# A token-routed FFN behind a graph convolution: second half of the first weights held back, and eleven unread matmuls

## What is computed

```python
logits = jnp.einsum('bsd,ed->bse', tgt, Wr) + br
top_v, top_i = jax.lax.top_k(logits, 2)          # 8 experts, 2 for each token
top_w = jax.nn.softmax(top_v, axis=-1)
...
h = jax.nn.relu(jnp.einsum('bsd,efd->bsef', tgt, W1) + b1)   # 1024 -> 512
o = jnp.einsum('bsef,edf->bsed', h, W2) + b2                 # 512 -> 1024
tgt2 = jnp.einsum('bsed,bse->bsd', o, router_w)
return _layer_norm(tgt + tgt2, gamma, beta)
```

## Time and profile before

| | us |
|---|---|
| median of 3 runs | 2134.6 |
| lowest, highest | 2126.74, 2134.81 |
| the profiled execution, its own time | 2129.83 |
| its span | 2128.1 |
| mean granted clock of TensorE | 0.974 |

### The profile page before, as it was taken

The page is one execution under the profiler, slowest core; times in us unless marked ns, Lnnn a source line. Parts: engine busy times, 40 slices in busy tenths (PEclk is TensorE's granted clock), DMA queues, the critical chain, the costliest instruction groups (busy, mean ns, idle before and its releaser), DMA issues. The chain is left out here.

```text
span 2128.1 us, 27953 instructions
## 1 busy us (share of the span) xinstructions
PE 2011.7 (95%) x9385; PEld 1600.0 (75%) x9385; DVE 1252.4 (59%) x2316; ACT 986.1 (46%) x1541; POOL 924.6 (43%) x813
## 2 busy tenths in 40 slices
PE   7999999999999999999989999899889949999994
PEld 6777777777777777887868767677568748888883
DVE  7589868952222222216989988888978852222237
ACT  3211122222222222227999999999934313333346
POOL 0000036555565655406777877878700012221226
PEclk9999999999999999999999999999989959999997
DMA  5322277777777777768788989989947679999747
GB/s 188 105 81 79 71 241 254 253 264 257 248 262 249 251 252 252 255 204 292 262 315 286 324 283 330 338 303 319 329 152 225 201 294 330 312 295 310 239 133 166
DMA packets 156360, 521.55 MB, mean 245 GB/s; under 512 B 31362, under 2 KB 31746, under 8 KB 154186
## 3 DMA queue, kind: packets, MB, share of 16 engines
q1 hardware_dynamic: 83706, 308.63, 41.6%
q0 software_dynamic: 72528, 211.35, 32.4%
HBM read 385.49 MB, written 156.25 MB: 255 GB/s over the span
## 5 line engine op out<-in xcount | busy, mean ns | idle before, releaser
L221 PE MATMUL psum<-w_hi,xnT_hi 128*128 128x512 f32 (+1 forms) x1592 | 420.2, 398 | 9.9 <-issue 5.0
L221 PE MATMUL psum<-w_lo,xnT_hi 128*128 128x512 f32 (+1 forms) x1592 | 419.5, 394 | 0.0
L221 PE MATMUL psum<-w_hi,xnT_lo 128*128 128x512 f32 (+1 forms) x1592 | 413.0, 394 | 0.0
L590 ACT ACTIVATE work<-psum 128x512 f32<-128x512 f32 (+1 forms) x150 | 89.9, 599 | 673.0 <-PE psum L221 673.0
L924 POOL DMA_INDIRECT sorted_rows<-acc x313 | 340.6, 1088 | 116.2 <-issue 84.9
L221 PEld LDWEIGHTS psum<-w_hi,xnT_hi 128*128 128x128 f32 (+1 forms) x1592 | 292.2, 186 | 80.5 <-issue 9.1
L221 PEld LDWEIGHTS psum<-w_lo,xnT_hi 128*128 128x128 f32 (+1 forms) x1592 | 295.4, 186 | 74.4
L221 PEld LDWEIGHTS psum<-w_hi,xnT_lo 128*128 128x128 f32 (+1 forms) x1592 | 294.6, 185 | 71.9
L1040 POOL DMA_INDIRECT w_hi<-y_rows,sort_row x168 | 228.2, 1358 | 63.2 <-issue 39.7
L1040 POOL DMA_INDIRECT w_lo<-y_rows,sort_row x164 | 216.5, 1320 | 62.6 <-issue 42.0
L1125 DVE SCALAR_TENSOR_TENSOR w_hi<-w_hi,sort_recip,y_hi 128x1024 fp32r<-128x1024 f32 x168 | 213.7, 1283 | 37.0 <-ACT y_hi L1086 32.2
(11 more groups left out here) (383 smaller groups left out, 2644.8 us busy)
## 6 DMA issues: line engine op xcount, KB each, us to landing
split_experts<-acc SPq DMA_DIRECT2D x128, 512.0 KB, 4.2
ring<-split_experts SPq DMA_DIRECT2D x16, 4096.0 KB, 15.6
w_raw<-in_wchunks SPq DMA_DIRECT2D x86, 512.0 KB, 5.3
y_rows<-work SPq DMA_DIRECT2D x144, 256.0 KB, 2.8
acc<-in_wchunks SPq DMA_DIRECT2D x64, 512.0 KB, 6.0
work<-local_rows SPq DMA_DIRECT2D x26, 384.0 KB, 4.2
acc<-in_bias SPq DMA_DIRECT2D x10, 512.0 KB, 5.8
sorted_rows<-acc POOLq DMA_INDIRECT x313, 4.5
```

The source lines that it names most:

```text
L221: i = pe.matmul(to[:rm, :], x_[:, k, m * P:m * P + rm], w_[:, s, k * HALF:(k + 1) * HALF], start=(n == 0), stop=(n == 3 * KD - 1))
L590: act.activation(stage_y[:rows(m), t % 4, :], bank[t % 4][:rows(m), :], ACT.Copy)\
```

## The change

SP issues only half 0 in the routing. Half 1 leaves in the expert stage, behind the two b2 copies and behind a wait for token tile 0; the halves 2 and 3 follow behind a wait for tile 1, ahead of the loop that raises `w1_ready` and `w2_ready`. TensorE gets eleven float32 matmuls of 128x128 by 512 columns into `bank[7]`, which nobody reads: four ahead of the list matmuls, two behind them, three at the end of the routing stage and two ahead of token tile 0.

```diff
+        def keep_busy(pe, n):
+
+            for _ in range(n):
+                pe.matmul(bank[7], ident[:, :], acc[:, 0, 0:HALF], start=True, stop=True)
...
             def _(sp):
-                for n in range(2):
-                    load_half(sp, n, n * P)
+                load_half(sp, 0, 0)
...
             def _(pe):
+                keep_busy(pe, 4)
                 for c in range(COLS):
...
                 i.then_inc(list_done, 1)
+                keep_busy(pe, 2)
                 pe.wait_ge(weight_hot, 1)
...
                 i.then_inc(weight_done, 1)
+                keep_busy(pe, 3)
...
                     sp.dma_start(o_s[at:at + E, 0, :], b2).then_inc(b2_in, 16)
+                sp.wait_ge(t_in[0], 16)
+                load_half(sp, 1, P)
+                sp.wait_ge(t_in[1], 16)
+                for n in range(2, RING):
+                    load_half(sp, n, n * P)
                 for n in range(HALVES_E):
-                    if n == 2:
-                        for i in range(2):
-                            sp.wait_ge(t_in[i], 16)
-                    if 2 <= n < RING:
-                        load_half(sp, n, n * P)
                     if n == RING:
...
                 pe.sem_inc(s1_done)
                 pe.sem_inc(s2_done)
+                keep_busy(pe, 2)
                 token_tile(0)
```

## The result

The changed kernel took 2140.0 us in the median of 12 runs against 2134.6 us for the kernel before (12 runs): a ratio of 1.0029 with a 95% interval of 1.0015 to 1.0043, about 6 us slower. That is within 0.5%, but clear of no change, and 1 us above the range given.

What follows compares the result with a forecast made beforehand. TensorE was taken to bound the kernel, jointly with the DMA engines until about 1894. DMA time of 5 us lost and 5.1 won back cancelled the 8.4 us head start: 0 us gained, 2131 us predicted, range 2119 to 2139.

Steps and rivals of the forecast that it cites:

- Tile 0's transposes: TensorE's first token transposes: to start at 1738.3 instead of 1743.59, the tile having already landed.
- Layer one over: End of the first block's layer one on TensorE: 1746.9, against 1755.3 before.
- Head start: TensorE's lead after the first layer: 8.4 us, or 3.7 us with the clock still low.
- the former hole: DMA engines in 1771 to 1776, share 0.38 before: to be near 1.00, winning back 3.1 us.
- Idle DMA time: DMA engines: 5 us lost at the front, 5.1 us won back by 1880, net 0.1 us.
- Token waits: TensorE's waits for token gathers: to sum to about 11 us instead of 2.4, the last ending near 1894.
- The DMA share while the half is held: DMA engines between about 1732 and 1738, with only the gathers running: share below 0.5.
- all three gathers in: Start of the expert stage: tile 0 lands at 1735.0, the others 1.3 and 2.6 us later, all before 1736.5.
- The prediction's sum: TensorE's head start of 8.4 us set against DMA time lost and won back: net change 0 us, -3 to +3.
- TensorE keeps going from 1894, so the end moves by the same: After the last token wait, near 1894, TensorE alone counts; the end shifts as that wait's end does.
- rival (B): Held half shifts the weight stream and pauses before 1894 vanish: +5 us, +11 with a stretched iteration; chance 0.11.
- Rival (C): Clock stays low through the unread matmuls: +2.5 us by TensorE alone, up to +8 with DMA time; chance 0.04.

Runs made afterwards that it cites:

- e1: The whole change without the eleven unread matmuls; ratio 1.0028 to the kernel before.
- e4: The whole change with the ten beta accumulates on every second block instead of blocks 0 to 9; ratio 1.0004 to the kernel before.
- e3: The whole change with SP holding weight half 7 back until TensorE has finished layer one of block 8; ratio 1.0033 to the kernel before.
- e2: The kernel before plus the eleven unread matmuls, with its DMA order kept; ratio 1.0004 to the kernel before.
- e14: The change without the eleven matmuls, halves loaded by four DMAs of 8 KB rows, w1_ready raised early; ratio 1.0008 to the kernel before.
- e9: The whole change with every weight half loaded by four DMAs of 8 KB rows; ratio 1.0018 to the kernel before.
- e13: The whole change, halves loaded by four DMAs of 8 KB rows, w1_ready raised as soon as half 0 is in; ratio 0.9999 to the kernel before.
- e15: The kernel before with each half loaded by four DMAs of 8 KB rows, second run; ratio 0.9960 to the kernel before.

## Why the prediction was wrong

**Right, by its own steps.** Tile 0's transposes: 1739.97 less the 1.32 us by which the stage began later is 1738.7 (forecast 1738.3). Layer one over at 1748.8 - 1.3 = 1747.5 (1746.9). Head start 7.8 us (8.4). The gathers landed in 4.3 to 5.0 us (4.2). The list matmuls delayed nothing in this execution. DMA share 1.10 in the former hole (near 1.00). Idle DMA time in the first 140 us of the stretch, added up from the shares of windows of 2 us: 2.9 us before, 4.2 after, so 1.3 lost on balance (0.1). Token waits 10.6 us (about 11); that this sum came out is partly luck, since e1 with nearly the same head start has 9.1 and e4 with the same one 5.6.

**Off without consequence.** The DMA share while the half is held was to be below 0.5. Over 1731 to 1741 it is 0.54, but in the six microseconds named (1733.3 to 1739.3 here) it is 0.72: the engines stood still for 3 us ahead of the gathers (0.01 and less from 1730.3 to 1733.3), and the gathers filled them more than was thought. The prediction also has all three gathers in before the stage starts at 1736.5, while its own figures put the third at 1737.6. It landed 4.8 us behind its issue at 1734.85, so at 1739.6, behind the stage's start at 1737.84; TensorE needed only tile 0.

**Wrong.** The prediction's sum took a wait of TensorE at its own length. That step failed. The waits grew by 8.1 us and so took the 7.8 us and hardly more, but the head start was paid back in two waits of 3.95 and 3.41 us, and behind each of them TensorE ran some matmuls at 1.2 GHz; the two blocks took 1.85 and 1.83 us more than their waits. The sum puts this term, 3.7 us, at nothing; with it, it gives the +3.5 us of the profiles. The small waits of the kernel before (1.0, 0.5, 0.9 us) have no such mark. Over all profiled executions, a token wait of up to 1.7 us cost its length and at most 0.3 us more (0.5 in one block of e3, which had a second wait besides); of two waits of 1.9 us one cost 0.2 us more and one 1.8; every wait of 2.1 us or more cost 1.7 to 3.2 us more. The clock's part is read from rows and was not isolated by a run of its own.

The step "TensorE keeps going from 1894, so the end moves by the same" held, but the last token wait ended at 1872, not near 1894: the loss came in two blocks in a row and early. Of the prediction's rival (B) the sign came true, and its mechanism in part: in the profiled execution the short interval came two places later, but in e1 it did not, and the time was as long. Its price of 5 us came from lost DMA time, and the profiles show 3.5, the runs 6. I gave it 0.11, and against it counted idle time as won back. Most of it was won back, by the weights, which were not what TensorE waited for next. Rival (C) had a chance of 0.04 and its effect appeared in two of eleven executions; e1, which has no such matmuls, is as slow as the change, so it is no large part of the result.

The range failed by 1 us at 2139 for two reasons: the missing term, and its centre, which leaned on one profiled execution of 2129.8 us that had no long wait, while the runs of before lie between 2127 and 2146 us.

What stays open: why the runs differ by 6 us and the profiles by 3.5. One pair of profiles can't settle 2.5 us, since a stretch moves by 3 us from one execution to the next, and e2's, with the DMA order of before and a wait of 4.24 us, shows that long waits are not the change's alone. Open too is why e14's profiled execution waits for weights three times, 10.4 us in all and 4.64 of them as late as block 21, which makes its stretch 417.4 us where its ratio is 1.0008.

## What to carry to other kernels

Where the DMA engines are full behind a gap in the work, as here at a share of 0.98 to 1.00, a transfer held back isn't free: its time is owed and comes back as a wait on whatever is scarce next. Before trading transfers against each other, make the turns fair: here loading a 32 KB row in four pieces was worth 0.4%, with no other change. A wait of TensorE should be priced with what the clock takes behind it: three waits of 1 us cost 0.2 to 0.3 us each beyond their length here, one of 3.01 us in e1 cost 1.8.

## What the hardware showed

- A GpSimd scatter beside a weight half in 32 KB rows landed in up to 17.8 us, beside the same bytes in 8 KB rows in at most 11.5 us.
- SP's issues are not always 0.42 us: twelve in a row of 1 MB each took 15.2 us in e9 and 16.0 in e13, eight took 4.44 us in e15, three of 4 MB took 1.30 us.
- During the first four unread matmuls the clock rose (1.00 from 4 us of the stretch on, 0.81 over 1720 to 1731 in the kernel after). In all eleven executions it fell back to 0.50 to 0.54 from 10 to 12 us, around the end of the 28-column matmuls; in nine it was at 1.00 again from 14 us on, in two it stayed down until the stage was over.
